# Cross-attention and a quantised feed-forward on one core: less filler and another order in the prologue, two rows of maxima by DMA, a weight quarter on another queue, and batch 7's maxima one tile ahead

## What is computed

```python
x = x + xattn(layernorm(x), ctx_768, Wq, Wk, Wv, Wout, bout)   # 8 heads of 64
x = x + ffn(layernorm(x), clip_x, clip_down, w_gate, w_up, w_down)

def xattn(x, context, Wq, Wk, Wv, Wout, bout):
    q, k, v = x @ Wq, context @ Wk, context @ Wv               # split in 8 heads
    attn = softmax(q @ k.T * 64 ** -0.5)
    return (attn @ v) @ Wout + bout
```

## Time and profile before

| | |
|---|---|
| median of 3 runs | 181.56 us (181.48 to 181.96) |
| the profiled execution | 181.43 us, of which 179.4 us are its span |
| busy | PE 96%, DVE 81%, ACT 75%, POOL 71%, weight loads 79% |
| chain that ended last | PE 91%, DVE 5%, ACT 1%, issue 1% |

### The profile page before, as it was taken

How to read it: one execution, slowest core, us unless ns; L and a number is a source line. 1 busy time by engine, 2 the same in 40 slices (tenths; PEclk the granted TensorE clock), 3 DMA queues, 4 the chain that set the end, 5 groups by cost and what they waited for, 6 DMA issues and landing times.

```text
span 179.4 us, 2941 instructions
## 1 busy us (share of the span) xinstructions
PE 172.7 (96%) x889; PEld 142.6 (79%) x889; DVE 144.7 (81%) x341; ACT 133.8 (75%) x284; POOL 127.8 (71%) x135
## 2 busy tenths in 40 slices
PE   7999999999999999999999999999999999999783
PEld 2865678888888889888888898888888888898431
DVE  6596578969984896899987968999979869958784
ACT  3477989878869995778878857788877677855732
POOL 5698399989995888689987866899788675533010
PEclk9999999999999999999999999999999999999999
DMA  5767900180017000800071008100400000000001
GB/s 151 224 167 214 257 27 4 13 242 8 0 44 213 0 4 2 249 5 2 0 215 45 2 0 230 31 0 0 130 0 2 4 0 0 0 0 5 0 0 51
DMA packets 8331, 11.41 MB, mean 64 GB/s; under 512 B 4276, under 2 KB 6516, under 8 KB 8316
## 3 DMA queue, kind: packets, MB, share of 16 engines
q1 hardware_dynamic: 7900, 10.83, 22.8%
q10 hardware_dynamic: 416, 0.40, 0.7%
HBM read 10.97 MB, written 0.23 MB: 62 GB/s over the span
## 4 chain that ended last, share of the span: by engine, by line
PE 91%; DVE 5%; ACT 1%; issue 1%; DVEq 0%; POOL 0%; ACTq 0%; POOLq 0%
PE p_n L1057 11%; PE p_sw L1038 11%; PE p_m L1016 11%; PE p_n L1065 11%; PE p_sw L1030 11%; PE p_n L1059 11%; PE p_sw L1031 11%; PE p_n L966 2%; PE p_n L1073 1%; PE p_n L1093 1%; PE p_m L1133 1%; DVE h_flat L924 1%; PE p_m L1000 1%; PE p_n L1000 1%; PE p_sw L1133 1%
## 5 line engine op out<-in xcount | busy, mean ns | idle before, releaser
L370 POOL TENSOR_TENSOR e_lo<-e_full,e_hi 125x448 fp32r<-125x448 f32 x48 | 55.7, 1160 | 26.0 <-ACT e_full L537 24.8
L534 ACT ACTIVATE e_hi<-p_sw 125x448 fp32r<-125x448 f32 x96 | 52.2, 543 | 23.9 <-PE p_sw L1038 23.3
L675 DVE TENSOR_REDUCE chunk_max<-p_m 112x1 f32<-112x500 f32 x84 | 55.6, 673 | 16.3 <-PE p_m L1016 15.4
L1030 PE MATMUL p_sw<-q_hi,ctxT_lo 96*125 96x448 f32 x96 | 36.3, 378 | 0.0
L1057 PE MATMUL p_n<-e_hi,ctx_hi 125*128 125x448 f32 x96 | 35.5, 370 | 0.0
L1038 PE MATMUL p_sw<-q_hi,ctxT_hi 97*125 97x448 f32 x96 | 35.4, 369 | 0.0
L1065 PE MATMUL p_n<-e_lo,ctx_hi 125*128 125x448 f32 x96 | 35.1, 366 | 0.0
L1031 PE MATMUL p_sw<-q_lo,ctxT_hi 96*125 96x448 f32 x96 | 35.1, 365 | 0.0
L1059 PE MATMUL p_n<-e_hi,ctx_lo 125*96 125x448 f32 x96 | 35.0, 364 | 0.0
L690 DVE TENSOR_TENSOR e_lo<-p_n,e_hi 125x448 fp32r<-125x448 f32 x48 | 29.6, 617 | 4.0 <-ACT p_n L551 3.8
L1016 PE MATMUL p_m<-ctxT_hi,q_hi 96*112 96x500 f32 x84 | 32.2, 393 | 0.0
(11 more groups left out here) (255 smaller groups left out, 206.2 us busy)
## 6 DMA issues: line engine op xcount, KB each, us to landing
ctx_in<-ctx_d SPq DMA_DIRECT2D x8, 504.0 KB
ctxT_in<-ctxT_d SPq DMA_DIRECT2D x7, 562.5 KB, 5.9
ctxT_in<-ctxT_d SPq DMA_DIRECT2D x3, 187.5 KB, 4.4
ctx_in<-ctx_d SPq DMA_DIRECT2D x8, 58.5 KB
q_hi<-maxima SPq DMA_DIRECT2D x28, 0.4 KB, 1.9
wout<-wout_d SPq DMA_DIRECT2D x1, 256.0 KB, 7.4
wqkT<-wqkT_d SPq DMA_DIRECT2D x1, 224.0 KB, 4.4
wvT<-wvT_d SPq DMA_DIRECT2D x1, 192.0 KB, 6.7
```

The source lines that it names most:

```text
L370: pool.tensor_tensor(e_lo[:, k, :], e_full[:, k, :], e_hi[:, k, :], ALU.subtract)\
L534: act.activation(e_hi[:, k, :], p_s[n % 2][0:KT, 0:HQ], ACT.Exp, scale=SCALE)\
L675: dve.reduce_max(chunk_max[:, c // NM, c % NM:c % NM + 1], p_mb[c % NM][0:GQ, 0:MC], AX.X)\
L1030: pe.matmul(o, ctxT_lo[b % 2][:, keys], q_hi[0:C, b, :], start=True, stop=False)
```

## The change

- The filler behind the first folded weights shrinks from 5 to 3 matmuls, that behind the transpose from 9 to 5, and the 3 between batch 0's first two chunks go.
- The three chunks of group 0 run in one go, ahead of `first_queries(1)`; before, the third came behind it.
- Rows 0 and 1 of batch 0's maxima go by DMA from SP's queue, as in the loop; PE's `row(0)`, `row(1)` and ACT's `row_copy(0)` go.
- Weight quarter 1 is issued by SP ahead of the context's pieces, and no longer by ACT.
- `q_banks` of heads 6 and 7 change places: head 6 takes the bank of head 3, head 7 that of head 4. The waits follow.
- Batch 7's chunks ride one tile earlier: chunks 2 and 3 with tile 0 of batch 6, then 4 to 11 with tiles 1 to 8, none with tile 9.

```diff
 def chunks_at(b, t):
...
+    if b == B - 2:
+        return [(b + 1, c) for c in ((2, 3) if t == 0 else (t + 3,) if t + 3 < CHUNKS else ())]
     return [(b + 1, t + 2)]
...
-        q_banks = [p_s[1], p_s[0], p_mb[0], p_mb[1], p_o[1], p_mb[2], p_o[1], p_mb[1]]
+        q_banks = [p_s[1], p_s[0], p_mb[0], p_mb[1], p_o[1], p_mb[2], p_mb[1], p_o[1]]
-        row_banks = [p_s[0], p_mb[2]]
...
-            sp.dma_start(wqkT[:, 0, :], wqkT_d[:, 0, :]).then_inc(qk_loaded[0], 16)
+            for j in range(2):
+                sp.dma_start(wqkT[:, j, :], wqkT_d[:, j, :]).then_inc(qk_loaded[j], 16)
...
+            for g in range(G - 2):
+                sp.wait_ge(s.first_max_made, g + 1)
+                sp.dma_start(q_hi[C:C + 1, 0, g * GQ:(g + 1) * GQ].bitcast(F32), maxima[0][:, g:g + 1])\
+                    .then_inc(max_moved[0], 16)
             wait_ctxT_lo(sp, 0)
...
             act.dma_start(x_in[:, 1:PAIRS, :], x_d[:, 1:PAIRS, :]).then_inc(s.x_loaded, 16)
-            act.dma_start(wqkT[:, 1, :], wqkT_d[:, 1, :]).then_inc(qk_loaded[1], 16)
...
             ctxT1_hi(0)
-            row_copy(0)
             split_q(0)
             split_q(1)
-            row_copy(1)
+            row_copy()
...
             weights_qk(0).then_inc(s.wqk_made, 1)
-            busy(5, p_x, 128)
+            busy(3, p_x, 128)
...
-            busy(9, p_x, 128)
+            busy(5, p_x, 128)
...
                 if b == 1 and c < 3:
-                    pe.wait_ge(s.last_q_lo_made, (1, 6, 4)[c])
+                    pe.wait_ge(s.last_q_lo_made, (1, 5, 4)[c])
...
                 elif h == 1:
-                    pe.wait_ge(max_moved[0], 32)
+                    pe.wait_ge(s.xnT_copied, 2)
...
-                elif h == 6:
-                    pe.wait_ge(s.last_q_lo_made, 3)
-                elif h == 7:
-                    pe.wait_ge(s.last_q_lo_made, 2)
+                elif h >= 6:
+                    pe.wait_ge(s.last_q_lo_made, h - 4)
...
             busy(2, p_s[0], 128)
-            first_max_chunks(0, (0,))
-            busy(3, p_s[0], 128)
-            first_max_chunks(0, (1,))
+            first_max_chunks(0)
             pe.wait_ge(s.wqk_copied, 2)
             pe.wait_ge(s.first_q_full_made, 1)
             first_queries(1)
-            first_max_chunks(0, (2,))
             weights_qk(2)
...
             pe.wait_ge(s.xnT_copied, 2)
-            row(0)
-            row(1).then_inc(s.row_made, 1)
             query(0)
```

More of the change, by code:

```diff
@@ L471, in _, with row_copy @@
             act.activation(pair0(e_full, slice(4, H)), by_batch(p_s[1][0:C, 0:HQ]), ACT.Copy).then_inc(s.first_q_full_made, 1)
[L473 to L477, removed]
+            def row_copy():
+                act.wait_ge(s.row_made, 1)
+                act.activation(q_hi[C:C + 1, 0, 2 * GQ:HQ], p_mb[2][C:C + 1, 2 * GQ:HQ], ACT.Copy).then_inc(max_moved[0], 32)
             def split_q(h):
@@ L987, in _, with first_max_chunks @@
             pe.transpose(p_mb[2][:, 0:TOK], xn[:, 0, :], ident[0:TOK, 0:TOK]).then_inc(s.xnT_made, 1)
-            busy(9, p_x, 128)
-            def first_max_chunks(g, pieces=range(NM)):
+            busy(5, p_x, 128)
+            def first_max_chunks(g):
                 pe.wait_ge(s.first_q_hi_made, g + 1)
@@ L994, in first_max_chunks @@
                     pe.wait_ge(s.first_max_made, g - 1)
-                for k in pieces:
+                for k in range(NM):
                     if g == 1 and k == 2:
@@ L1136, in row @@
             def row(g):
-                return pe.matmul(row_banks[g // 2][C:C + 1, g * GQ:(g + 1) * GQ], maxima[0][:, g:g + 1], ident[0:GQ, 0:GQ],
+                return pe.matmul(p_mb[2][C:C + 1, g * GQ:(g + 1) * GQ], maxima[0][:, g:g + 1], ident[0:GQ, 0:GQ],
                                  start=True, stop=True)
```

## The result

| | before | changed |
|---|---|---|
| median of 20 runs each | 181.56 us (181.22 to 182.08) | 181.28 us (180.72 to 185.32) |
| ratio, 95% interval | | 0.9977 (0.9966 to 0.9988) |
| profiled execution, its span | 181.43, 179.4 | 180.72, 178.8 |

The ratio is 0.42 us off 181.56, or 181.14. The interval leaves out 1, so the gain is clear of noise, but it is smaller than the 0.3% from which the prediction would have called it faster. Five of the changed kernel's 20 runs took 184.8 to 185.3 us and none of before's did; this ratio and those further down leave such runs out, and the experiments come back to them.

A forecast was written before the change was run, and what follows sets the result against it. PE was taken to bound the kernel: 0.30 us from the prologue (weights earlier) plus 0.17 from the banks, other terms 0, made 0.47 off 181.43, or 180.96; the median, 0.13 above, was forecast at 181.1 us, range 180.7 to 181.7.

## What to carry over

Before you say that an engine runs without a break, compare starts with the spacing of the same pair elsewhere, and ask whether one of its instructions waits for the work that the change moves. A gain ahead of a step that waits for a load is spent there, and landing times scatter by more than the gain, so such a term needs several traces. Filler in a prologue is not idle time: with less of it the changed order was no faster in most runs and 4 us slower in some. The version with the new order and 5 and 9 filler matmuls (0.9959, none over 181.34) is the one to keep.

## What was not expected of the hardware

- The same kernel's third piece of context landed at 7.16 and at 7.46; over all the variants 6.11 to 7.47. In both the landing set the third cast and with it tile 0, which differed by 0.3 us as well.
- Half clock can last with PE busy: three chunks in a row at 1.59 instead of 0.94 up to 17 us, with one gap of 0.17 on record between 3.8 and 17 us. No run here shows why. The row of the granted clock shows a fall (0.50 from 10 to 14 us without the filler of 3 and 5) but not a late first rise (1.00 with chunks of 0.5 each). In the views only the spacing of equal matmuls tells that.
- ACT's copy and exponential overlap the next instruction by about 0.1 (the copy 0.43 long, the next 0.33 later; the exponential 0.54 long, the copy 0.47 later), so listed idle times on ACT understate what a predecessor costs.
